# Cross totals with TensorE's epsilon, maxima first in the queue, context turned by DMA

## The reference

```
x = layernorm(x + causal_attention(x))            # 16 heads of 16
Pn = rmsnorm(ctx, input_w); k = Pn @ Wk.T; v = Pn @ Wv.T
repeat 3 times:                                   # slots = x at the start
    q = rmsnorm(slots, slot_w) @ Wq.T
    attn = softmax(q @ k.T / 16, over the slots)  # slots compete for each context row
    attn = attn / (sum over the context of attn + 1e-6)
    slots = gru(attn @ v, slots)
x = layernorm(x + slots)
x = layernorm(x + experts(x))                     # 4 of 16 experts by sigmoid gates
```

## Time and profile before

| | us |
|---|---|
| median of 3 runs | 668.17 (667.05 to 669.31) |
| the profiled execution | 666.62 |
| its span | 664.9 |
| mean granted TensorE clock | 0.982 |
| busy: TensorE (PE) | 621.7 (93%) |
| VectorE (DVE) | 493.7 (74%) |
| ScalarE (ACT) | 327.0 (49%) |
| GpSimd (POOL) | 225.2 (34%) |

### The profile page before, as it was taken

How to read it: one execution, slowest core, us unless ns; L and a number is a source line. 1 busy time by engine, 2 the same in 40 slices (tenths; PEclk the granted TensorE clock), 3 DMA queues, 4 the chain that set the end, 5 groups by cost and what they waited for, 6 DMA issues and landing times.

```text
span 664.9 us, 13964 instructions
## 1 busy us (share of the span) xinstructions
PE 621.7 (93%) x5064; PEld 565.3 (85%) x5064; DVE 493.7 (74%) x1039; ACT 327.0 (49%) x734; POOL 225.2 (34%) x274
## 2 busy tenths in 40 slices
PE   5988998998999999999999999999999998899996
PEld 4766787776767989999899998999989988799996
DVE  4755474674764788879888799887999888767653
ACT  5444553553575355655556555565566644231320
POOL 9402332432453251422223232232312213352543
PEclk9799898997999999999999999999999999999999
DMA  8634646357400040010000000000000000042240
GB/s 283 203 103 146 173 135 190 93 173 217 121 18 1 1 160 0 2 33 2 0 0 0 32 0 0 0 0 0 0 1 1 1 1 1 16 147 82 80 157 34
DMA packets 31374, 43.34 MB, mean 65 GB/s; under 512 B 3072, under 2 KB 18912, under 8 KB 31328
## 3 DMA queue, kind: packets, MB, share of 16 engines
q1 hardware_dynamic: 31328, 42.73, 21.1%
HBM read 29.39 MB, written 13.21 MB: 64 GB/s over the span
## 4 chain that ended last, share of the span: by engine, by line
PE 56%; DVE 13%; issue 13%; DMA 5%; SPq 5%; POOL 4%; ACT 3%; DVEq 0%; POOLq 0%; ACTq 0%
PE bank L448 26%; PE bank L2171 11%; PE bank L1991 4%; POOL hid_hl L801 3%; DMA k_rows<-k_hl 3%; PE bank L1891 2%; DMA q_op<-negT 2%; PE bank L1977 1%; PE bank L456 1%; PE bank L1849 1%; PE bank L2008 1%; SPq L519 1%; PE bank L1856 1%; PE bank L1872 1%; PE bank L2000 1%
## 5 line engine op out<-in xcount | busy, mean ns | idle before, releaser
L448 PE MATMUL bank<-slots_hl,whhT_hl 128*128 128x256 f32 x864 | 113.1, 284 | 0.0
L448 PEld LDWEIGHTS bank<-slots_hl,whhT_hl 128*128 128x128 f32 x864 | 105.5, 188 | 2.4 <-ACT gate_z L1104 1.0
L1293 DVE TENSOR_REDUCE neg_max<-bank 128x2 f32<-128x512 f32 (+1 forms) x96 | 65.7, 690 | 55.2 <-PE bank L1858 41.3
L2171 PE MATMUL bank<-attn_hl,vg_hl 128*128 128x256 f32 x864 | 105.7, 280 | 0.1
L2171 PEld LDWEIGHTS bank<-attn_hl,vg_hl 128*128 128x128 f32 x864 | 100.9, 188 | 4.3 <-ACT attn_hl L815 3.9
L870 ACT ACTIVATE pT<-bank 128x512 f32<-128x512 f32 x96 | 56.9, 598 | 57.7 <-PE bank L1872 41.7
L682 POOL TENSOR_SCALAR_AFFINE_SELECT pT<-pT 128x512 f32<-128x512 f32 x64 | 40.6, 638 | 117.5 <-ACT pT L870 117.4
L696 POOL TENSOR_TENSOR sq<-sq 128x256 f32<-128x256 f32 x24 | 18.1, 754 | 170.6 <-ACT sq L1089 130.3
L801 POOL TENSOR_TENSOR hid_hl<-hid,hid_hl 128x512 fp32r<-128x512 f32 x32 | 40.9, 1303 | 25.8 <-ACT hid_hl L815 25.7
L448 PE MATMUL bank<-x2T_hl,keys_hl 128*128 128x256 f32 x384 | 48.6, 284 | 0.0
L448 PE MATMUL bank<-values_hl,hid_hl 128*128 128x256 f32 x384 | 47.8, 281 | 0.3 <-DVE x L1567 0.3
(11 more groups left out here) (212 smaller groups left out, 1298.2 us busy)
## 6 DMA issues: line engine op xcount, KB each, us to landing
gate_rows<-gate_mem SPq DMA_DIRECT2D x48, 128.0 KB, 3.1
q_rows<-q_hl SPq DMA_DIRECT2D x21, 256.0 KB
k_rows<-k_hl SPq DMA_DIRECT2D x21, 256.0 KB
q_op<-q_rows SPq DMA_DIRECT2D x28, 192.0 KB, 3.2
k_op<-k_rows SPq DMA_DIRECT2D x14, 384.0 KB, 4.4
x_in<-in_x_dram SPq DMA_DIRECT2D x8, 256.0 KB, 6.6
c_in<-in_ctx_dram SPq DMA_DIRECT2D x8, 256.0 KB, 4.8
out_dram<-y_out SPq DMA_DIRECT2D x8, 256.0 KB, 2.8
```

The lines of the kernel that those rows point to most:

```text
L448: mm = pe.matmul(dst, left(a), right(b), start=first and n == 0, stop=last and n == 2, skip_group_check=True)
L1293: dve.tensor_reduce(dst, src, AX.X, ALU.max, negate=True).then_inc(max_ok, 1)
L2171: mm = pe.matmul(halves(b)[:, m, :], vg_hl[:, j, v_part, 3 * t + r, q:q + P], attn_hl[:, j, at_part, t, :], start=n == 2 and a + m + t == ...
```

## The change

The totals' sum starts with a product of a column of ones (broadcast) by a column that holds epsilon / 64 in 64 rows and 0 in the others, both fp32r; the sum itself is multiplied by ones instead of 1/256; so the bank holds total + epsilon, and VectorE takes the reciprocal from it directly. The bank is now handed on by the reciprocal (`it_ok`). The SyncE program issues the maxima ahead of the rest at places 0 and 4, and last, as before, at places 2 and 6. The context is loaded a second time, transposed on the host (`ctxT`), into the same buffer once the squares are summed, and ACT and VectorE split it from there; the transposes on TensorE, their semaphore and their banks go. `q_op` and `k_op` have 97 rows instead of 128, and the waits on `rows_ok` go.

```diff
-        q_op = sb("q_op", [P, 2, 2, H // 2, T], F32R, where=sq_op)
+        q_op = sb("q_op", [K_ROWS + 1, 2, 2, H // 2, T], F32R, where=sq_op)
...
-            cT, kT, *vg = ((0, 1, 3, 2, 0), (1, 0, 3, 6, 7))[j]
-            jobs = [(("cT", j), cT, cT_lo, 2, 2 + j + 1), (("kT", j), kT, kT_lo, 2, 2 + j + 1)]
+            kT, *vg = ((1, 3, 2, 0), (0, 3, 6, 7))[j]
+            jobs = [(("kT", j), kT, kT_lo, 2, 2 + j + 1)]
...
-            return [(("tt", u), 2, tt_ok, UNITS, u + 1), (("r", u), 4, r_ok, UNITS, u + 1), ...
+            return [(("tt", u), 2, it_ok, UNITS, u + 1), (("r", u), 4, r_ok, UNITS, u + 1), ...
...
+            def turned_context(i, j):
+                sp.wait_ge(c_sq, due(2, i, j + 1))
+                sp.sem_inc(passed, 1)
+                sp.dma_start(c_in[:, j, :, :], rows(ctxT[i * 2 + j, :, :], NC)).then_inc(cT_arr[j], 16)
...
+                if quad in (QUADS - 6, QUADS - 5):
+                    turned_context(0, quad - (QUADS - 6))
+                if place in (0, 4) and 0 <= quad // 2 + 1 < 2 * B:
+                    maxima(quad // 2 + 1)
                 if place == 0:
...
-                if quad % 2 == 0 and 0 <= quad // 2 + 1 < 2 * B:
+                if place in (2, 6) and 0 <= quad // 2 + 1 < 2 * B:
                     maxima(quad // 2 + 1)
...
             def load_context(i):
                 for j in range(2):
-                    sp.wait_ge(cT_mm, due(2, i, j + 1, back=1))
-                    sp.sem_inc(passed, 1)
-                    sp.wait_ge(c_sq, due(2, i, j + 1, back=1))
+                    sp.wait_ge(cT_lo, due(2, i, j + 1, back=1))
                     sp.sem_inc(passed, 1)
                     sp.dma_start(c_in[:, j, :, :], ctx[i * 2 + j, :, :].rearrange("(t p) d -> p t d", p=P)).then_inc(c_arr[j], 16)
+                for j in range(2):
+                    turned_context(i, j)
...
             def context_text_hi(r, j, first=False):
-                act.wait_ge(cT_mm, due(2, r, 2 + j + 1))
+                act.wait_ge(cT_arr[j], due(1, r, 2, step=16))
                 act.wait_ge(vg_mm, due(6, r, 6 + 3 * j))
-                copy(cT_hl[:, HI, :, :], halves(context_bank(("cT", j), first))).then_inc(cT_hi, 1)
+                copy(cT_hl[:, HI, :, :], c_in[:, j, :, :]).then_inc(cT_hi, 1)
...
             def totals(i, u):
                 dve.wait_ge(tt_mm, due(UNITS, i, u + 1))
-                dve.tensor_scalar(tot[:, :], bank[2][:, 0:T], float(D), RMS_EPS, ALU.mult, ALU.add).then_inc(tt_ok, 1)
-                dve.wait_ge(tt_ok, due(UNITS, i, u + 1))
-                dve.reciprocal(inv_tot[:, :], tot[:, :]).then_inc(it_ok, 1)
+                dve.reciprocal(inv_tot[:, :], bank[2][:, 0:T]).then_inc(it_ok, 1)
...
             def totals(i, u, first=False):
                 j = u % 2
                 b = free_bank(i, ("tt", u), first)
+                if first:
+                    pe.wait_ge(eps_ok, 5)
+                pe.matmul(bank[b][:, 0:T], one_r[:, :].to_broadcast([P, P]), eps_r[:, :].to_broadcast([P, T]), start=True, stop=False)
                 pe.wait_ge(z_ok, due(UNITS, i, u + 1))
-                pe.matmul(bank[b][:, 0:T], mean_col[:, :].to_broadcast([P, P]), tot[:, :], start=True, stop=True).then_inc(tt_mm, 1)
+                pe.matmul(bank[b][:, 0:T], one_col[:, :].to_broadcast([P, P]), tot[:, :], start=False, stop=True).then_inc(tt_mm, 1)
```

More of the change, by code:

```diff
@@ L66, in after, with decoder_layer @@
         engine.wait_ge(signal, count)
-def decoder_layer(nc, x, xT, ctx, w_qkv, w_proj, wq, wk, wv, wihT, whhT, eselT, keys, values, cols, lines, out):
+def decoder_layer(nc, x, xT, ctx, ctxT, w_qkv, w_proj, wq, wk, wv, wihT, whhT, eselT, keys, values, cols, lines, out):
     stack = ExitStack()
@@ L94, in decoder_layer @@
         warm = sb("warm", [P, 1])
+        one_r = sb("one_r", [P, 1], F32R)
+        eps_r = sb("eps_r", [P, 1], F32R)
+        one_col = sb("one_col", [P, 1])
+        eps_col = sb("eps_col", [P, 1])
         qk_w_hl = sb("qk_w_hl", [P, 2, NC, D], F32R)
@@ L155, in decoder_layer @@
         x_in = sb("x_in", [P, 2, NT, D], where=s1)
-        k_op = sb("k_op", [P, 2, H // 2, T], F32R, where=s1)
+        k_op = sb("k_op", [K_ROWS + 1, 2, H // 2, T], F32R, where=s1)
         v_aug = sb("v_aug", [P, 3, NT, H, 2 * DH], where=s1)
@@ L268, in decoder_layer @@
         spot_in, spot_ok = sem("spot_in"), sem("spot_ok")
-        rows_ok = sem("rows_ok")
+        eps_ok = sem("eps_ok")
         set_mm, set_q, set_k = sem("set_mm"), sem("set_q"), sem("set_k")
@@ L284, in decoder_layer @@
         c_sq, c_mean, c_rstd, c_kept = event("c_sq", 2), event("c_mean", 2), event("c_rstd", 2), event("c_kept", 1)
-        cT_mm, cT_hi, cT_lo = event("cT_mm", 2), event("cT_hi", 2), event("cT_lo", 2)
+        cT_arr = [event(f"cT_arr{j}", 1, 16) for j in range(2)]
+        cT_hi, cT_lo = event("cT_hi", 2), event("cT_lo", 2)
         kT_mm, kT_hi, kT_lo = event("kT_mm", 2), event("kT_hi", 2), event("kT_lo", 2)
@@ L294, in decoder_layer @@
         si_ok, sh_ok = event("si_ok", UNITS), event("sh_ok", UNITS)
-        tt_mm, tt_ok, it_ok = event("tt_mm", UNITS), event("tt_ok", UNITS), event("it_ok", UNITS)
+        tt_mm, it_ok = event("tt_mm", UNITS), event("it_ok", UNITS)
         at_ok, at_hi, at_lo = event("at_ok", UNITS), event("at_hi", UNITS), event("at_lo", UNITS)
@@ L379, in mid @@
         def mid(u):
-            return [(("tt", u), 2, tt_ok, UNITS, u + 1), (("r", u), 4, r_ok, UNITS, u + 1), (("z", u), 5, zt_ok, UNITS, u + 1),
+            return [(("tt", u), 2, it_ok, UNITS, u + 1), (("r", u), 4, r_ok, UNITS, u + 1), (("z", u), 5, zt_ok, UNITS, u + 1),
                     (("hn", u), 6, hb_ok, UNITS, u + 1)]
@@ L653, in _ @@
             for batch in range(2):
-                pool.memset(f32(k_op[K_ROWS:, batch, :, :]), 1.0).then_inc(consts, 1)
+                pool.memset(f32(k_op[K_ROWS:K_ROWS + 1, batch, :, :]), 1.0).then_inc(consts, 1)
             pool.wait_ge(consts, 16)
@@ L658, in _ @@
             pool.wait_ge(consts, 19)
-            for e in range(2):
-                pool.memset(f32(q_op[K_ROWS:, 0, e, :, :]), 0.0).then_inc(rows_ok, 1)
-            pool.wait_ge(rows_ok, 2)
+            pool.memset(one_col[:, :], 1.0).then_inc(eps_ok, 1)
+            pool.memset(eps_col[:, :], RMS_EPS / 64).then_inc(eps_ok, 1)
+            pool.wait_ge(eps_ok, 2)
+            pool.tensor_copy(one_r[:, :], one_col[:, :]).then_inc(eps_ok, 1)
+            pool.tensor_copy(eps_r[:, :], eps_col[:, :]).then_inc(eps_ok, 1)
+            pool.wait_ge(eps_ok, 4)
+            pool.tensor_tensor(eps_r[64:P, :], eps_col[64:P, :], f32(eps_r[64:P, :]), ALU.subtract).then_inc(eps_ok, 1)
+            pool.wait_ge(eps_ok, 5)
             def rstd(i, var, ev, std, k, slot):
@@ L1346, in context_text_lo @@
                 dve.wait_ge(cT_hi, due(2, r, 2 + j + 1))
-                sub_hi(cT_hl[:, LO, :, :], halves(context_bank(("cT", j), first)), cT_hl[:, HI, :, :]).then_inc(cT_lo, 1)
+                sub_hi(cT_hl[:, LO, :, :], c_in[:, j, :, :], cT_hl[:, HI, :, :]).then_inc(cT_lo, 1)
             def context_keys_lo(r, j, first=False):
@@ L2024, in first_context @@
             def first_context(quad):
-                if quad == QUADS - 4:
-                    context_text(-1, 0, True)
-                elif quad == QUADS - 3:
+                if quad == QUADS - 3:
                     context_keys(-1, 0, True)
@@ L2175, in text @@
                     if last:
-                        b, read, count = LAST_TEXT[j], (ms_ok, tt_ok)[j], due(UNITS, i, UNITS)
+                        b, read, count = LAST_TEXT[j], (ms_ok, it_ok)[j], due(UNITS, i, UNITS)
                     else:
@@ L2188, in cross @@
                     inputs(u)
-                    if u == 4 and not last:
-                        context_text(i, 0)
                     if u + 1 < UNITS:
@@ L2306, in laid_out @@
     return {
-        'x': of('x'), 'xT': of('x').reshape(PAIRS, 2 * T, D).transpose(0, 2, 1), 'ctx': of('ctx_1024'), 'w_qkv': _np.stack([w_qkv[0], w_qkv[1], w_qkv[2][:, order]]),
+        'x': of('x'), 'xT': of('x').reshape(PAIRS, 2 * T, D).transpose(0, 2, 1), 'ctx': of('ctx_1024'),
+        'ctxT': of('ctx_1024').transpose(0, 2, 1), 'w_qkv': _np.stack([w_qkv[0], w_qkv[1], w_qkv[2][:, order]]),
         'w_proj': of('L0_attn_w_proj')[order],
```

21 lines of the change are left out of this document (6 added, 15 removed).

## The result

The changed kernel takes 674.12 us (median of 4 runs, 672.70 to 676.64) against 667.61 (4 runs, 666.87 to 669.31) for the kernel before: a ratio of 1.0103, interval 1.0071 to 1.0136, slower by 6.5 us: one per cent, clear of no change but small. The forecast was 674.9, in a range of 665 to 680. The profiled execution took 673.41, its span is 671.7 (664.9 before), the mean granted clock 0.976 (0.982).

The account below looks back on a forecast made before the run. Attention was taken as bound by TensorE except for three negT waits, cross as TensorE and VectorE nearly level. 5.7+1.2+0.7-0.5+0-0.4 = +6.7 us on the profiled 666.62 gave 673.3; with 1.55 for the median, 674.9, range 665 to 680.

Parts of the forecast that it names:

- Place 0 delays what SP issues behind it: Attention, quads 8 and 16: SP stands for the maxima, so what is behind goes out 2.8 and 2.9 us later.
- Both stalls grow, +5.7: Attention, quads 12 and 20: TensorE's waits for negT lengthen, together by 5.7 us (3.3 to 7.8).
- Quad 26, +1.2: Attention: natural scores near quad 26 newly wait for late operands sent at quad 24, 1.2 us (0 to 1.6).
- Clock, +0.7: Attention: a longer stall may lower TensorE's granted clock further behind the second stall, 0.7 us.
- Context work beside the last quads, -0.5: End of attention: four context transposes leave TensorE twice, saving 0.5 us (0 to 1.2).
- Middle units: no gain: Cross: VectorE's saved copy only lengthens its mean-squares wait; the extra product adds 0.12 a unit, +1.1 us over three passes.
- The pass's gain is spent at bank 2: Cross, pass end: text(0) waits about 1.5 us for the reciprocal, leaving 0 for three passes (-4 to +2).
- Last pass, -0.4: Cross, last pass: four units gain nothing, the unit after them gains 0.4 us.
- Rival 1: Cross: VectorE's saved time passes through at text(0), bank 2; 665.0 us in all, chance 0.18.
- Rival 2: Attention: the queue's reorder costs nothing, as SP has slack and DMA catches up; 667.3 us, chance 0.10.
- rival 3: Attention: only SP's pace counts, 3.3 for both stalls, no quad 26 wait or clock loss; 670.6 us, chance 0.14.
- rival 4: Attention: every cost at its upper bound, plus an operand wait at quad 14; 680 us or more, chance 0.10.

Follow-up runs that it names:

- b: The kernel before with only SP's order changed, maxima first at places 0 and 4: 676.95 us, ratio 1.0151.
- f: The changed kernel with the maxima first at place 0 alone, last at places 2, 4 and 6: 671.92 us, ratio 1.0140.
- j: The changed kernel with SP's order of before and without the product that adds epsilon: 663.92 us, ratio 0.9998.
- d: The changed kernel with SP's order of before and the banks of a pass's two text transposes exchanged: 659.78 us, ratio 0.9879.
- k: The changed kernel with the text transposes' banks exchanged and the maxima issued by ScalarE instead of SP: 663.45 us, ratio 0.9949.
- a: The changed kernel with SP's order of before, maxima last at every even place: 662.01 us, ratio 0.9960.
- g: The changed kernel with the maxima first at place 4 alone, last at places 0, 2 and 6: 663.83 us, ratio 0.9982.

## Why the prediction came out as it did

It was right in sign, and to 0.8 us in size, but so close a hit is luck: two errors in it cancelled. Attention lost 9.9 us where the sum had 7.1, and the cross passes gave back 2.2 where it had 0.

- **Place 0 delays what SP issues behind it.** Right, and shown by b, f and the chain. Predicted shift of place 2's operands 2.8, measured 2.9, or 3.3 counted from negT; the turned scores of quad 12 moved by 3.1.
- **Both stalls grow, +5.7.** The shift was right, the place wrong: negT's waits stayed 2.8 us. The step priced one thing that place 2 sends and passed over `k_op`, sent 2.7 us ahead of the pair and wanted by the natural scores, which come first in a quad. The new idle is 3.13 and 3.34 there: 6.5 for the two. So one sign of being right, waits of 5 to 7 us for negT, did not come.
- **Quad 26, +1.2.** Measured 1.95 at the weight load, 1.68 at the product.
- **Clock, +0.7.** Mis-sized for the profiled execution: about +2.3, with 10 us at 0.50 behind each of the two quads, and 6 us at 0.72 behind quad 26, which was priced without clock. It is not a fixed price of the stalls: b, with the same places and as much idle time, lost no more to the clock than the kernel before (6.1 against 6.2), and f less (5.2). That a longer stall can only add half-clock time was not borne out by these two.
- **Context work beside the last quads, -0.5.** Not settled: kernels with the same attention code differ by 2.4 us there.
- **Middle units: no gain.** Right. The wait for the mean squares grew from 0.23 to 0.54 as it should. That the product adds 0.12 to each was wrong: j shows 0. So was the 0.06 for reading PSUM: 1749 against 1753 ns.
- **The pass's gain is spent at bank 2.** The wait of about 1.5 us is there (1.39). But not all of the gain is spent: about 0.7 us a pass is left where 0 was forecast: the seventh reciprocal comes 1.33 earlier (19.86 to 18.53 from the sixth), and only 0.67 is lost behind it (16.18 to 16.85). The first part was foreseen: a reciprocal at 307.55 instead of 308.89 is the 1.33. What the term left out is the copy in the unit behind: the prediction had VectorE as the bound "into the next pass", and there its 0.42 us count in full. The other 0.24 is that the second statistics came that much sooner than reckoned. Term of the sum: 0, measured -2.2 for the three passes, within its bounds. One of its signs of being wrong, passes clearly under 82 us, did come (81.56).
- **Last pass, -0.4.** Its first units kept 11.85; the stage behind the last reciprocal was 0.9 shorter, but it varies by 3.7 us among kernels that share its code (127.0 to 130.7), so nothing is shown.
- **Rival 1 (VectorE's saving passes through)** was refused for the right reason; d is what it would have taken. **Rival 2 (the reorder is free)** fell with b. **Rivals 3 and 4:** the waits alone exceeded rival 3's bound, and the full price of rival 4 wasn't reached.

## What to carry to other kernels

When a wait is moved forward in an in-order issuing queue, read for each place both how long the queue will stand and whether what is queued behind leads to a stall: standing for the same 2 us or so went with some 10 us at place 0 and with nothing that could be measured at place 4. When a copy out of a bank is removed, the bank's next writer waits for the slower reader that took over, so give that writer another bank, and count the copy's time as saved where its engine has no wait behind it. After a stall is taken away, look at what the engine wants next: here it arrived sooner at a transfer that hadn't landed yet.

## What the runs showed of the hardware

- A VectorE reciprocal of 128x256 fp32 costs the same from PSUM (1749 ns) as from SBUF (1753 ns).
- One issue of the maxima on SP's queue took between 0.57 us (f, at 88.56) and 1.66 us (at 108.97, right behind writes of q rows). One `k_op` transfer of 384 KB landed 4.1 to 7.2 us after its issue in the kernel before (median 4.4), 7.58 us after it in k and 8.95 in a, these two issued right behind writes of k rows and loads of q rows.
- The length of a stall alone did not tell whether the granted clock fell. At quad 4 a stall of 2.08 us was followed by 0.84 over 64 to 75 us in the kernel before; stalls of 1.52 (the changed kernel), 2.06 (f) and 2.33 us (g) at the same place were followed by 1.00.
- Identical attention code gave first reciprocals 2.4 us apart (227.15 to 229.57), and run times of the kernel before spread over up to 8.5 us in one set of 25 (661.62 to 670.15), where the first four runs of it stayed within 2.5.
